# Two gated cross-attention and feed-forward layers on one core: eight groups written out in a straight line, the second attention by query chunk beside the last down product, and the first normalisation moved into its steps

## What is computed

```python
x = x + tanh(g_xattn[0]) * L0_xattn(layernorm(x), ctx)   # one head over 77 keys: softmax((x W + b)(ctx W + b)) ctx
x = x + tanh(g_ffn[0])   * L0_ffn(layernorm(x))          # ternary weights, RMS norm, 512 -> 2048, exact gelu, RMS norm, 2048 -> 512
x = x + tanh(g_xattn[1]) * L1_xattn(layernorm(x), ctx)   # 16 heads of 32 over 77 keys, Wq, Wkv, Wout with biases
x = x + tanh(g_ffn[1])   * L1_ffn(layernorm(x))          # NVFP4 fake quantisation of x and hidden, silu(gate) * up, down
```

## Time and profile before

| | us |
|---|---|
| median of 3 runs | 1810.36 (1810.17 to 1814.83) |
| the profiled execution | 1809.43 |
| its span in the profile | 1807.6 |
| PE busy in it | 1353.0 (75%) |
| DVE busy | 1422.8 (79%) |
| ACT busy | 692.1 (38%) |
| POOL busy | 240.5 (13%) |

### The profile page before, as it was taken

How to read it: one execution, slowest core, us unless ns; L and a number is a source line. 1 busy time by engine, 2 the same in 40 slices (tenths; PEclk the granted TensorE clock), 3 DMA queues, 4 the chain that set the end, 5 groups by cost and what they waited for, 6 DMA issues and landing times.

```text
span 1807.6 us, 24307 instructions
## 1 busy us (share of the span) xinstructions
PE 1353.0 (75%) x8120; PEld 699.1 (39%) x8120; DVE 1422.8 (79%) x2437; ACT 692.1 (38%) x2105; POOL 240.5 (13%) x197
## 2 busy tenths in 40 slices
PE   5044747799787978698778978797879886988663
PEld 3021315344453436343533345343634453434321
DVE  6988896878787687778687878768778878786695
ACT  2113206451464227432645146422734164425210
POOL 1002200131003200230013100320013001310000
PEclk9556868899899989999889999999989999999888
DMA  9165761042102320141004210232023200420011
GB/s 350 66 238 156 193 143 36 7 88 63 44 1 61 68 59 14 35 87 53 26 7 88 60 48 1 61 68 59 14 35 73 68 25 7 88 59 24 7 29 47
DMA packets 267433, 120.08 MB, mean 66 GB/s; under 512 B 244090, under 2 KB 244602, under 8 KB 265750
## 3 DMA queue, kind: packets, MB, share of 16 engines
q1 hardware_dynamic: 267286, 118.27, 25.7%
HBM read 49.04 MB, written 8.39 MB: 32 GB/s over the span
## 4 chain that ended last, share of the span: by engine, by line
issue 43%; DVE 26%; PE 21%; DMA 3%; ACT 3%; SPq 2%; POOL 2%; POOLq 0%; DVEq 0%; ACTq 0%
PE bank L1074 15%; PE bank L1163 5%; DVE amax L825 2%; DVE pair L834 2%; DVE th L867 2%; DVE hid L830 2%; SPq L303 1%; ACT region L534 1%; DMA hqt<-pair 1%; DVE pair L842 1%; DVE pair L849 1%; DVE hid L871 1%; DVE pair L844 1%; DVE sc L796 1%; DVE stats L685 1%
## 5 line engine op out<-in xcount | busy, mean ns | idle before, releaser
L1163 PE MATMUL bank<-w_dn,region 128*128 128x512 fp8e4 x1024 | 243.1, 386 | 36.8 <-DMA region<-region 36.8
L1074 PE MATMUL bank<-w_up,xt 128*128 128x512 fp8e4 x1024 | 245.6, 388 | 32.8 <-ACT region L498 17.5
L1074 PE MATMUL bank<-w_gate,xqt 128*128 128x512 bf16 x512 | 147.2, 415 | 127.9 <-DVE th L867 84.1
L507 ACT ACTIVATE th<-bank,half_cg 128x512 f32<-128x512 f32 x128 | 88.0, 687 | 347.4 <-PE bank L1074 347.4
L425 POOL TENSOR_TENSOR region<-g,region 128x512 f16<-128x512 f32 x128 | 177.8, 1394 | 298.9 <-ACT region L498 291.1
L867 DVE SCALAR_TENSOR_TENSOR th<-th,bank 128x512 f32<-128x512 f32 x128 | 87.6, 685 | 133.5 <-ACT th L507 133.5
L534 ACT ACTIVATE region<-bank,nm 128x77 f32<-128x77 f32 x512 | 160.2, 346 | 67.6 <-DVE nm L913 67.6
L1074 PE MATMUL bank<-w_down,hqt 128*128 128x512 bf16 x512 | 132.4, 418 | 56.2 <-DMA hqt<-pair 56.2
L495 ACT ACTIVATE g<-bank 128x512 f32<-128x512 f32 x128 | 76.4, 597 | 245.4 <-PE bank L1074 186.3
L1163 PEld LDWEIGHTS bank<-w_dn,region 128*128 128x128 f16 x1024 | 101.1, 99 | 162.4 <-issue 45.1
L1074 PEld LDWEIGHTS bank<-w_up,xt 128*128 128x128 f16 x1024 | 101.2, 100 | 161.5 <-issue 51.8
(11 more groups left out here) (206 smaller groups left out, 2469.8 us busy)
## 6 DMA issues: line engine op xcount, KB each, us to landing
xin<-in_x SPq DMA_DIRECT2D x16, 512.0 KB, 4.0
out_x<-x SPq DMA_DIRECT2D x16, 512.0 KB, 3.0
region<-in_w_up_t SPq DMA_DIRECT2D x1, 4096.0 KB, 12.8
hid<-in_gate_w SPq DMA_DIRECT2D x4, 1024.0 KB, 5.3
x<-in_gate_w SPq DMA_DIRECT2D x4, 1024.0 KB, 6.3
hid<-in_up_w SPq DMA_DIRECT2D x4, 1024.0 KB, 5.2
x<-in_up_w SPq DMA_DIRECT2D x4, 1024.0 KB, 5.6
hid<-in_down_w SPq DMA_DIRECT2D x4, 1024.0 KB, 4.8
```

Of the source, the lines that this page charges most:

```text
L507: eng.activation(th[:, u % 2, :], bank[4][:, :], ACT.Tanh, scale=half_cg[:, :]).then_inc(sg["th"], 1)
L1074: last = mm(out, lhs, rhs, start=(n == 0), stop=(n == len(pairs) - 1))
L1163: last = mm(bank[2 + t % 2][:, :], ht[i][:, t % 2, f, :], w_dn[:, f, :], start=(f == 0 and i == 0), stop=(f == KF - 1 and i == 1))
```

## The change

Groups in a straight line: the five hardware loops become Python loops over groups, the register arithmetic and some counters that only the loops had are gone, and the prologue, the loop and the copy after it become one list. The second attention goes by query chunk: the score of tile 0, chunk c waits only for `ql` of chunk c, and no longer for the last down product. `down4` of tile 3 moves into step 2 of phase A, in bank 3, ahead of that step's scores; its `out4` is in step 4 on DVE. The `out4` of tile 2 goes from slot 28 to slot 31. The quantisation of tile 3 takes three slots in place of two (27, 28, 29), so that `ql` of chunk 1 now comes ahead of its last part. `norm1` is taken apart: statistics of two tiles each in steps 0 and 1, the normalisation in step 2, and all of `stage1` starts two steps later: START1 goes from (1, 2, 7, 8) to (3, 4, 9, 10), VAR2_AT from 15 to 17, NORM2_AT from 17 to 19, T2_AT from 18 and 19 to 20 and 21, UP_AT from 20, 21, 22 to 22, 23, 24. STEPS stays 26, and X4_STEPS stay at 21 to 24.

```diff
-START1 = (1, 2, 7, 8)
+START1 = (3, 4, 9, 10)
+STATS1_AT = {0: (0, 1), 1: (2, 3)}
+NORM1_AT = 2
+LATE_DOWN, LATE_OUT = 2, 4
...
-SLOT_NORM1 = SLOT_Q + 2
...
-POST_AT = {TILE_AT[t] + (10 if t < TILES - 1 else 7): t for t in range(TILES)}
-SLOTS = max([SLOT_Q + NC] + [s + 2 for s in POST_AT]) + 1
+QUANT_AT[TILE_AT[-1] + 5], QUANT_AT[TILE_AT[-1] + 6] = (TILES - 1, (3,)), (TILES - 1, (4,))
+DOWN4_AT = {TILE_AT[t] + 11: t for t in range(TILES - 1)}
+OUT4_AT = {TILE_AT[0] + 12: 0, TILE_AT[1] + 12: 1, SLOT_Q + NC: 2}
+SLOTS = SLOT_Q + NC + 1
...
-            with sp.Fori(0, GROUPS - 2) as g:
-                turns(g, g + 1, g + 2)
-            turns(GROUPS - 2, GROUPS - 1, None)
-            turns(GROUPS - 1, None, None)
+            for g in range(GROUPS):
+                turns(g, g + 1 if g + 1 < GROUPS else None, g + 2 if g + 2 < GROUPS else None)
...
             def phase_a(g3, g1):
                 if g1 is not None:
+                    root(1, g1)
                     want(pool, "var2", g1)
...
             def stage1(g, n):
 
+                if n in STATS1_AT:
+                    if n == 0:
+                        want(dve, "xin", g)
+                    for t in STATS1_AT[n]:
+                        tile_stats(1, g, xin, t)
+                    if STATS1_AT[n][-1] == TILES - 1:
+                        norm_stats(1, g)
+                if n == NORM1_AT:
+                    norm(1, g, xin)
...
                     if g3 is not None:
                         attend(g3, n)
+                    if g3 and n == LATE_OUT:
+                        out4(g3 - 1, TILES - 1, 3)
                     if g1 is not None:
                         stage1(g1, n)
...
-                    if s == SLOT_NORM1 and g1 is not None:
-                        norm1(g1)
...
-                        if s - 2 in POST_AT:
-                            out4(s4, POST_AT[s - 2])
+                        if s in OUT4_AT:
+                            out4(s4, OUT4_AT[s])
...
-            def down4(g, t):
-                want(pe, *(("out4", g, t) if t else ("p3l", g)))
+            def down4(g, t, b=7):
+                if b == 7:
+                    want(pe, *(("out4", g, t) if t else ("p3l", g)))
+                else:
+                    want(pe, "qh", g + 1)
                 want(pe, "hqt", g, 16 * (t + 1))
...
-                    if n == 0:
-                        want(pe, "ql", g)
+                    if t == 0:
+                        want(pe, "ql", g, c + 1)
+                    if n == 0 and g:
+                        want(pe, "hid", g - 1)
...
             def phase_a(g3, g1):
                 for n in range(STEPS):
+                    if g3 and n == LATE_DOWN:
+                        down4(g3 - 1, TILES - 1, 3)
                     if g3 is not None:
                         attend(g3, n)
...
-            with pe.Fori(0, GROUPS - 2) as g:
+            for g in range(GROUPS - 1):
                 phase_a(g, g + 1)
                 phase_b(g + 1, g)
             g = GROUPS - 1
-            phase_a(g - 1, g)
-            phase_b(g, g - 1)
             phase_a(g, None)
```

More of the change, by code:

```diff
@@ L565, in _ @@
             phase_b(0, None)
-            with act.Fori(0, GROUPS - 2) as g:
+            for g in range(GROUPS - 1):
                 phase_a(g, g + 1)
@@ L880, in quant4, with out4 @@
                 quantise(buf[:, :], h_sc[:, :], h_g[:, :], parts, sg["hq"])
-            def out4(g, t):
+            def out4(g, t, b=7):
                 want(dve, "dn4", g, t + 1)
-                eng.scalar_tensor_tensor(x3[:, t, :], bank[7][:, :], kd[:, :], x3[:, t, :], ALU.mult,
+                eng.scalar_tensor_tensor(x3[:, t, :], bank[b][:, :], kd[:, :], x3[:, t, :], ALU.mult,
                                          ALU.add).then_inc(sg["out4"], 1)
@@ L1033, in _ @@
             scalar(kd[:, :], inv[:, 2:3], tg[:, 3:4], ALU.mult)
-            phase_b(0, None, 1)
+            phase_b(0, None)
             dve.wait_ge(sm["piece_read"], len(FP4_PIECES))
             dve.wait_ge(sm["wt_done"], WT_DONE)
-            pro = steps[1]
-            with dve.Fori(0, GROUPS - 2) as g:
-                steps[0], steps[1] = g * DVE_STEPS + pro, 0
+            for g in range(GROUPS - 1):
                 phase_a(g, g + 1)
-                phase_b(g + 1, g, g + 2)
-                assert steps[1] == DVE_STEPS, steps[1]
-            steps[0], steps[1] = (GROUPS - 2) * DVE_STEPS + pro, 0
+                phase_b(g + 1, g)
             g = GROUPS - 1
-            phase_a(g - 1, g)
-            phase_b(g, g - 1, None)
             phase_a(g, None)
@@ L1179, in gate_up @@
                     last.then_inc(sg["gate" if i == 0 else "gu"], 1)
-            def down4(g, t):
-                want(pe, *(("out4", g, t) if t else ("p3l", g)))
+            def down4(g, t, b=7):
[3 more added lines that the diff above has]
+                    want(pe, "qh", g + 1)
                 want(pe, "hqt", g, 16 * (t + 1))
-                product(bank[7][:, :], [(hqt[:, k, :], w_down[:, k, :]) for k in range(KF)]).then_inc(sg["dn4"], 1)
+                product(bank[b][:, :], [(hqt[:, k, :], w_down[:, k, :]) for k in range(KF)]).then_inc(sg["dn4"], 1)
             def query(g, c):
@@ L1232, in attend @@
                         want(pe, "p3l", g, m - 1)
+                    elif m == 1 and g:
+                        want(pe, "out4", g - 1, TILES - 1)
                     for j in range(HC):
@@ L1240, in attend @@
                         want(pe, "x3", g, t)
+                    elif g:
+                        want(pe, "out4", g - 1)
                     for k in range(KD):
@@ L1275, in phase_b @@
                             gate_up(s4, GU_AT[s])
-                        if s - 1 in POST_AT:
-                            down4(s4, POST_AT[s - 1])
+                        if s in DOWN4_AT:
+                            down4(s4, DOWN4_AT[s])
             phase_a(None, 0)
```

39 lines of the change are left out of this document (8 added, 31 removed).

## The result

The changed kernel takes 1821.47 us (median of 20 runs, 1819.73 to 1823.55). The kernel before, run beside it, has a median of 1812.72 us (20 runs, 1807.93 to 1823.49); beside the experiments, in three rounds, it had 1813.67, 1810.92 and 1814.64. Medians here are of all runs, and the ratios leave out one run, of e6_norm2_late at 1883.47 us, in which the chip was in a slower state. The ratio is 1.0044 with an interval of 1.0033 to 1.0055, so the change makes the kernel about 8 us slower. The prediction was 1800.0, range 1779 to 1816: the time lies outside the range, and the sign was wrong.

The account below looks back on a forecast made before the run. No engine is full; time goes where one in-order engine stands before another ("issue", 43% of the span). Sum: 1809.4 - 21 + 15.0 - 2.8 - 1.5 = 1799.1 us in the profiled execution, so 1800.0 predicted, range 1779 to 1816.

Parts of the forecast that it names:

- The straight line: Hardware loops written out: looped copies become as short as the copy already written straight; 21 us saved, bounds 14 to 26.
- Rival D: Loop edges cost no more than their branch; straight line gives 0.5 us, 1820.5 us in all; chance 0.03.
- The border: Between attentions: the third row maximum comes 0.6 us behind down4, where it was 3.3; gain 2.1 us in each border.
- (5): Clock at the end of phase A: slow stretch moves from before gate to up(0) and w_o; +0.5 us, bounds -1.7 and +3.4.
- (1): First normalisation in phase A, steps 0 to 2: its scaling and out4 delay later maxima; cost 1.3 us, between 0 and 2.6.
- (2): Steps 11 and 15: DVE waits behind PE's w_o product, stalls 4.1 us against 2.03; cost 2.1, between 0 and 3.
- (3): End of phase A: x_lo moves behind quantisation parts, statistics to this side; x4 starts 1.9 us earlier by that.
- (4): End of phase A: up(0), ahead of the last w_o, waits for x_lo; x4 to w_o 10.8 us, not 7.45; cost 3.3.
- rival C: PE at 1.2 GHz over up(0) and w_o of tile 3 in every copy: +3.4 us each, 1817.4 in all; chance 0.12.
- The first border and the last group: First border: earlier third maximum less phase A's cost, -2.8 us; last group: border gain less out4, -1.5 us.
- A: The moved order finds idle time and costs nothing: 1774.6 us, or 1775 to 1789 on the way there; chance 0.22.
- B: The whole of the moved order shows, +4.0 and +0.5 us in six copies: 1814.0; chance 0.25 for 1805 to 1816.

Follow-up runs that it names:

- e6_norm2_late: The kernel before with its loops written out straight, plus statistics, second normalisation, its transposes and first up products two steps later: 1824.25 us.
- e1: The kernel before with only its hardware loops written out straight on all engines, in the old order: 1786.76 us.
- e2: The kernel before with the loop written out on DVE alone, other engines keeping theirs: 1795.62 us.
- e7: The changed kernel with the first normalisation whole at the end of phase B, stage1 at its old steps and the late down product in step 1: 1788.49 us.
- e3: The changed kernel with x4's quantisation parts one step later, so that the four x_lo come ahead of them: 1773.55 us.
- e5: The changed kernel with 16 and 6 unread products on PE behind the transposes of steps 20 and 21, ahead of up(0): 1803.22 us.
- e9: e5 with 20 more unread products on PE ahead of gate unit 1: 1790.99 us.
- e8: e3 with 14 unread products on PE ahead of the late down product: 1758.06 us.

## Why the prediction was wrong

**The straight line: right in kind, and just over its upper bound.** Forecast -21, bounds 14 to 26; e1 gives -26.9. The 0.4 us for each of six bodies in the lower bound stood on no row. The straight copy of before was a fair sample of all copies, its clock of 0.98 included (e1: 0.97). I had discounted it for no row. The Trainium skill (Runtime: NRT & Kernel Launch, Instruction fetch mechanics) says that a taken branch out of the loaded window stalls for a fetch; the gaps of 2.2 to 2.6 us, and their absence in e1, agree with it. The about 0.1 us that the same skill gives a compare-and-branch (Advanced Engine Details and Errata, Control Flow Timing) is not the price of a loop's edge here: DVE's gaps are some twenty times that, and e2's 15.3 us lie on one engine's five edges and its loop body. Rival D is refuted.

**The border: the step right, its worth wrong.** The third maximum is 0.56 us behind down4 (forecast 0.6), and the lead against e1 is 33.5 - 31.4 = 2.1 us, as forecast. But e7 and e3 show that such a lead did not reach the end of a copy. That I carried it into the sum undiminished is one step that failed; the larger one is (5).

**(1), (2), (3): about right.** The stalls are 0.78 and 2.04 us, 2.8 in all against 4.1. x4 starts 79.0 after the third normalisation in the changed kernel and 80.8 in e1, 1.8 earlier, where -2.1 + 1.3 + 2.1 - 1.9 made 0.6 earlier. The hand count lost too much, as I had suspected, by 1.2 us.

**(4): right.** 10.8 us from x4 to w_o at full clock was forecast, and e5, with the clock up, has 10.6. In the changed kernel it is 12.3.

**(5): the term that failed.** I put the clock at +0.5 per copy, "near to even exchange", with a bound of +3.4. Keeping PE busy gave back 3.3 (e5) over up(0) and w_o, and 1.9 more (e9) behind the wait for gate unit 1: 5.2. So the clock term was ten times too small. Three things were wrong in it.
- There was no exchange. I reasoned that filling the idle time ahead of the gates with up(1) and up(2) would take the slow stretch there away. The wait before gate unit 0 did shrink (5.75 to 1.94), but the next wait, 5.17 us for DVE's th, had a slow stretch of 6.8 us behind it.
- I named rival C for one place and gave it 0.12. The place was right, up(0) and w_o, and so was its price of about 3.4 per copy. What spoke for it, the seven idle microseconds, was in the count of (4) already: up(0) goes late and PE has nothing but transposes before it. A wait of 5.3 us, eight transposes and a wait of 1.5 more didn't keep the clock. The earlier trace rows had shown the same after 4.9 and 5.75 us.
- I took (4) and (5) as separate. They are one: the same move that makes up(0) late also makes PE idle before it.

In the sum: forecast +2.5 in each of six copies, measured 6.7, which is 25 us. The straight line gave 6 us more than counted. The first border and the last group, forecast at -2.8 and -1.5, gave 2.7 together, 1.6 less (0.9 in the first copy, 1.8 in start and tail). 1800 + 25 - 6 + 1.6 = 1820.6. The third maximum of the first border came at 285.4, close to the 284.2 forecast.

**The chances.** The forecast, A and B together had 0.85, and each of them let the clock stay near where it was. It should have been the other way round: with two waits of over 5 us in the new order, full speed behind them was the case that needed a reason. The range ended at 1816 because the two upper bounds were never added: +4.0 for the queues and +3.4 for the clock make 7.4 per copy, and 6.7 was measured.

## What to carry to other kernels

When work is moved on an engine whose clock falls with idleness, price the move twice: the wait that it makes, and the half speed of what comes behind. Look for the product on the chain that stands behind the new wait. Here four DVE operations, moved behind x4 and three parts of a quantisation, cost 48 us, more than the hardware loops of five engines; with the order left as it was, filling PE's waits (e9) gave back 30 of them. And before a reordering is bundled with a straight line, run the two apart: the one gained 27 us and hid that the other lost 35, while moving one block back by one step (e3) turned that loss into a further gain of 13. Look at more than one copy, too: e6's profile is of its fastest run, and its middle copies alone would have halved the loss.

## What the runs showed of the hardware

- A hardware loop cost more than the gap at its edge. DVE showed 2.2 to 2.6 us of idle time at each of five edges, some 12 us, but making DVE's loop straight gave 15.3 us (10.7 to 19.4 by the interval) and all five engines' loops 26.9. How much of that is the jump, and how much the arithmetic in registers inside the loop, is not shown.
- "issue" on 43% of the chain of waits was worth 26.9 us, 1.5% of the time: a share of the chain says what stands last, and not what its removal brings.
- In the changed kernel the granted clock stayed at 0.50 for 10.2 us, from 1128.9 to 1139.1, through eight transposes, up(0) and most of w_o, with PE busy for 7.84 us of it.
- Extra matmuls made the kernel faster. 22 unread products per copy gave 18.3 us (e5), 20 more gave 12.2 (e9), and 14 at the border gave 15.5 (e8), where the down product went from 5.30 to 3.40 us. By the ratios these are 19.6, 11.4 and 10.9.
